# Third stage of a five-stage kernel: VectorE's skip term is moved ahead of its copies of the values

## The reference

```python
# 1: selective scan (state of 64 per column), with a skip term
proj = xn @ x_proj_w.T                      # xn: x normalised
delta, B_ssm, C_ssm = split(proj)
h = exp(dt * A) * h + dt * b * xn;  y = sum(h * c)      # step by step
out = (y + x * D_param) @ out_proj_w.T
# 2: of the mixture of experts only expert 0 reaches the output
out = x @ expert_w[0].T + expert_b[0]
# 3: linear attention with a data-dependent decay
w = sigmoid(xn @ Wx.T @ Ww.T + bw); k = xn @ Wk.T; v = xn @ Wv.T; r = sigmoid(xn @ Wr.T)
state = (1 - w) * state + k v^T;  out = r state;  y = out @ Wo.T
# 4: a routed spline on eight columns of each row
```

## Time and profile before

| | |
|---|---|
| time, median of 3 runs | 8359.2 us (8356.88 to 8362.91) |
| time of the profiled execution | 8361.57 us |
| its span, first to last instruction | 8359.7 us |
| granted TensorE clock, mean over the span | 0.953 |
| TensorE matmul busy | 7512.8 us (90%) |
| VectorE busy | 6668.3 us (80%) |
| ScalarE busy | 4668.4 us (56%) |
| GpSimd busy | 5670.6 us (68%) |
| DMA | 390.21 MB, mean 47 GB/s |

### The profile page before, as it was taken

One profiled execution on the slowest core, in us unless ns is written; L12 is line 12 of the kernel. 1 busy time (PEld: TensorE's weight loads), 2 busy tenths in 40 slices (PEclk: granted clock), 3 DMA queues, 4 the chain that ended last, 5 costly groups with the idle time before them and its releaser, 6 DMA issues. The chain is left out here.

```text
span 8359.7 us, 220056 instructions
## 1 busy us (share of the span) xinstructions
PE 7512.8 (90%) x75782; PEld 5505.6 (66%) x75782; DVE 6668.3 (80%) x8330; ACT 4668.4 (56%) x10568; POOL 5670.6 (68%) x3272
## 2 busy tenths in 40 slices
PE   8899999999999999999999997899999989999984
PEld 4577777777777777777777775444444446666653
DVE  7799999999999999999999996222222248888766
ACT  7787878787887788788787784111111112222220
POOL 1599999999999999999999995000000025545534
PEclk9999999999999999999999998999999988888885
DMA  6500000000000000000000001221111122222225
GB/s 213 142 16 0 16 16 0 16 16 0 16 16 5 11 16 16 0 16 16 0 16 16 0 5 68 74 77 70 70 70 70 67 96 78 75 77 76 78 73 163
DMA packets 198621, 390.21 MB, mean 47 GB/s; under 512 B 26273, under 2 KB 52321, under 8 KB 186977
## 3 DMA queue, kind: packets, MB, share of 16 engines
q1 hardware_dynamic: 189520, 370.71, 13.3%
q10 hardware_dynamic: 8976, 17.83, 0.6%
HBM read 208.72 MB, written 179.77 MB: 46 GB/s over the span
## 5 line engine op out<-in xcount | busy, mean ns | idle before, releaser
L494 POOL TENSOR_TENSOR scan_hc<-scan_h,scan_cb 128x1024 f32<-128x1024 f32 x2048 | 4776.0, 2367 | 103.0 <-PE scan_y L617 81.4
L659 DVE TENSOR_TENSOR_SCAN scan_h<-scan_a,scan_carry,scan_u 128x512 f32<-128x512 f32 x4096 | 4800.3, 1255 | 14.9 <-POOL scan_hc L494 7.8
L553 ACT ACTIVATE scan_a<-scan_dt,scan_aneg 128x512 f32<-128x512 f32 x4096 | 2658.4, 708 | 7.4 <-ACT scan_yo L533 7.4
L606 PE MATMUL scan_u<-scan_dg,scan_v 64*128 64x128 f32 x32768 | 2379.8, 285 | 313.3 <-DVE scan_h L659 269.5
L606 PEld LDWEIGHTS scan_u<-scan_dg,scan_v 64*128 64x128 f32 x32768 | 1990.4, 187 | 793.1 <-DVE scan_h L659 556.1
L617 PE MATMUL scan_y<-scan_ident,scan_hc 128*128 128x128 f32 x16408 | 2250.9, 280 | 14.3 <-ACT scan_yo L533 9.9
L617 PEld LDWEIGHTS scan_y<-scan_ident,scan_hc 128*128 128x128 f32 x16408 | 1757.6, 140 | 272.9 <-ACT scan_yo L533 15.7
L524 ACT ACTIVATE scan_dg<-scan_half,scan_bt 128x64 f32<-128x64 f32 x4096 | 1139.0, 341 | 4.8 <-DVE scan_onward L645 4.1
L164 POOL TENSOR_TENSOR mid_r<-mid_ve,mid_half_neg 128x4 f32<-128x4 f32 x32 | 32.4, 1012 | 1406.9 <-DVE mid_ve L132 916.5
L545 ACT ACTIVATE scan_carry<-scan_h,scan_onward 128x4 f32 (+1 forms) x1008 | 303.0, 301 | 933.3 <-DVE scan_h L659 933.2
L1163 POOL TENSOR_TENSOR core_joint<-core_own 128x32 f32<-128x32 f32 x64 | 17.4, 272 | 618.5 <-DVE core_own L1293 561.9
(11 more groups left out here) (206 smaller groups left out, 7248.2 us busy)
## 6 DMA issues: line engine op xcount, KB each, us to landing
scratch_y<-scan_yo ACTq DMA_DIRECT2D x17, 1024.0 KB, 4.3
pre_x<-in_x SPq DMA_DIRECT2D x16, 1024.0 KB, 5.7
scratch_dt<-pre_dt SPq DMA_DIRECT2D x16, 1024.0 KB, 5.9
scratch_vr<-pre_vr SPq DMA_DIRECT2D x16, 1024.0 KB, 4.7
scan_dt<-scratch_dt SPq DMA_DIRECT2D x16, 1024.0 KB, 5.3
scan_v<-scratch_vr SPq DMA_DIRECT2D x32, 512.0 KB, 7.6
mid_yr<-scratch_y SPq DMA_DIRECT2D x16, 1024.0 KB, 7.0
mid_x<-in_x SPq DMA_DIRECT2D x16, 1024.0 KB, 8.3
```

What stands on the lines that cost most here:

```text
L494: pool.tensor_tensor(hc[:, q].rearrange("p n (r j) -> p n r j", j=P), h[:, q].rearrange("p n (r j) -> p n r j", j=P), cb[:, bass.ds(b * NS ...
L553: ins = act.activation(a[:, q, n, :], dt[:, par, q, :], ACT.Exp, scale=aneg[:, q, bass.ds(m * 2 + n, 1)])
L606: mm = pe.matmul(u_ps[:, q % 2, g, k * HP:(k + 1) * HP, :], v[row, par, k, q, :], dg[row, buf, k], start=True, stop=True)
L659: ins = dve.tensor_tensor_scan(h[:, q, n, :], a[:, q, n, :], u_ps[:, q % 2, :, :, n].rearrange("p g t -> p (g t)"), carry[:, q, bass.ds(m ...
```

## The change

In VectorE's list of pieces the entry `(2, skips)` moves from the last place to the one ahead of `(0, values)`. In each of the turns 0 to 13 VectorE so issues the eight instructions of the skip term of chunk c+2, with their waits for `y_in` and `x_in`, before the four copies of the values of chunk c. Nothing else is changed; the calls ahead of the loop for chunks 0 and 1 come in the same order as before.

```diff
@@ -825,7 +825,7 @@
                     proj_steps.wait(dve, c, 3 * Q + j + 1)
                     dvep_steps.inc(dve.tensor_copy(vv[:, j, :], pb[:, j, :]))
             dve.wait_ge(consts, CONSTS * 16)
-            staggered(dve, NCH, [(1, first_sum), (1, second_sum), (0, keys), (1, more_norms), (0, values), (2, skips)])
+            staggered(dve, NCH, [(1, first_sum), (1, second_sum), (0, keys), (1, more_norms), (2, skips), (0, values)])
 
         @block.scalar
         def _(act):
```

## The result

| | before | after |
|---|---|---|
| median of the runs | 8359.37 us (8356.88 to 8362.91) | 8240.22 us (8237.45 to 8243.08) |
| profiled execution, its time | 8361.57 us | 8238.05 us |
| its span | 8359.7 us | 8236.1 us |

The ratio is 0.9857, with a 95% interval of 0.9840 to 0.9874: 119 us less. The forecast was 8241, in a range of 8236 to 8265.

A forecast was written before the change was run, and what follows sets the result against it. TensorE's chain was taken to bound the third stage, with waits for VectorE's skip term. Pause (6.46 us) and clock (2.03) sum to 8.49 us a turn, 14 times 118.9 us, giving 8241, range 8236 to 8265.

The forecast's parts named there:

- step 1: VectorE: the skip term fits its 8.78 us idle time with 3.2 us to spare, and could last until about 6019.
- step 5: TensorE's decays wait for the last value copy until 6021.60, hidden behind turn_y with 0.7 us to spare.
- Step 3: TensorE's pause before turn_y, waiting for the skip term, goes: 6.46 us a turn.
- Step 4: Without the pause TensorE's clock stays up: transposes of y save 1.71 us, decays 0.32, together 2.03 us a turn.
- Step 7: TensorE's jump back after every second turn, covered by the pause until now: taken as nothing, at most 25 us.
- Steps 2 and 6: Loads for the skip term land 59 us early; ScalarE's first sigmoid runs some 1 us late, hidden: both cost nothing.
- The clock was given back: Rival denied: the clock still falls at turn_y, so the gain is 90 us and the time 8269; chance 0.03.
- the back edge is not seen: Rival denied: TensorE's jump costs up to 3.58 us in seven turns, time 8265; chance 0.10, shared with late value copies.
- no DMA took the pause's place: Rival denied: late yr and x loads hold VectorE's value copies and the turn, some 8400 at 100 us; chance 0.01.
- the order did matter: Rival denied: something else, masked, holds TensorE at 6027, so the order does not matter; time 8359, chance 0.01.

The follow-up runs named there:

- e3: The changed kernel with the four skip-term instructions of L785 run three times instead of once, 5.5 us more on VectorE per turn: 8247.00 us.
- e4: The changed kernel with the four skip-term instructions of L785 run seven times instead of once, 16.5 us more on VectorE per turn: 8305.5 us.
- e1: The changed kernel with the skip term moved further ahead on VectorE, before the key copies: 8360.06 us.
- e2: The changed kernel with the skip term placed behind the third of the four value copies and ahead of the last: 8301.89 us.
- e11: The kernel before the change, with 7 extra matmuls of 512 columns on TensorE ahead of its wait for the skip term: 8336.08 us.
- e10: The changed kernel run once more with the same code: 8239.84 us.
- e5: The changed kernel with the skip term one place further ahead on VectorE, between the key copies and more_norms: 8246.0 us.
- e6: VectorE's order as in the kernel before; TensorE instead runs the first half of the decays ahead of turn_y: 8315.11 us.

## Why the prediction was right

**Steps 1 and 5, the place and the next wait.** As predicted: the skip term fits, 3.23 us are left, and the decays follow the last copy by 0.86 us, of which 0.15 is the semaphore's and 0.7 the room of step 5. e3 and e4 show the limit that step 1 gave: 5.5 us more cost no turn anything, 16.5 us more cost 2.37 us a turn, against 2.35 worked out from the same rows (2.47 as the mean of the two kinds of turn).

**Step 3, the pause.** 6.46 us a turn, and it is gone. e1, e2 and e4 bring it back in other lengths at the places that the order gives.

**Step 4, the clock.** 2.03 us a turn; e11 gets 1.96 without touching VectorE. The price holds for this pause only: 3.03 us behind 6.8 us at the reads, about 1.65 behind 2.85 us, where it fell at all. What sets the size isn't shown.

**Step 7, the back edge.** Priced at nothing, and it shows nowhere: `turn_y` of every second turn now follows the values across the jump with no gap (6.87 us from start to start in all turns), and from the fourth chunk on the distances are 90.50 to 90.53 us.

**Steps 2 and 6.** No wait for a load appears. ScalarE's sigmoid is 1 us late, as expected, and hidden.

**The sum.** From the first half of the values of turn 0 (5311.52 before, 5307.99 after) to the second half of those of turn 14 (6706.56 and 6584.01) the time shrank from 1395.04 to 1276.02 us, by 119.0; the prediction had 118.9. The two profiled executions differ by 123.5 us. The other 4.5 lie outside these turns: 3.5 ahead of them, mostly in the start of the stage, which e10 shows to vary by 4 us with the same code, and 1 behind them. No part of the change touches either. So the agreement of the turns is earned, term by term; that 8241 also met the median within 1 us is partly luck, since the time outside the turns varies by more than that.

**The rivals.** The clock was given back, the back edge is not seen, no DMA took the pause's place, and the order did matter (e1).

## What to carry to other kernels

When an engine that paces a stage waits for an engine that works through its list in order and is mostly idle, look at what stands in the idle engine's list ahead of the awaited work, and whether those pieces could be needed later: here eight instructions moved into 8.8 us of idle time were worth 119 us. The room of such a move is measured from the place where the first consumer of the pieces that are now behind comes, not from the visible idle time (3.2 us here, and 5.5 us more cost nothing). Price a pause of TensorE with what it does to the matmuls behind it, and price the calls ahead of the loop separately, where nothing covers a move (6 us in e5).

## What was not expected of the hardware

The clock did not need a long pause to fall. In e6 waits of 0.78 and 2.14 us, with 9 us of matmuls between them, were followed by the low level (0.50) in 13 of 14 turns, and the fall came while TensorE was already at work. In e4 waits of 1.73 and 0.35 us, 1.8 us of transposes apart, left it at the full level from the fourth chunk on. The Trainium skill, page "TensorE: Matmul & The Clock Gate", section "A second HAM failure mode: psum-queue depth-cycling", says that frequent micro-idles between groups can be enough. The prediction found nothing for it in the trace before, and for the kernel after that held; in e6 this trace agrees with it, at 1.8 us a turn. With one pause of 2.85 us (e2) the level fell in 11 of 14 turns of the same code.
